# Masking attention scores on VectorE instead of TensorE, with the steps of the loop written out

## The reference

```python
qkv = jnp.einsum('btc,oc->bto', x, w_qkv)            # x: 16 sequences of 512 tokens, 128 channels
q, k, v = ...                                        # 16 heads of 8 channels
attn = jnp.einsum('bhqd,bhkd->bhqk', q, k) / math.sqrt(DK)
mask = jnp.abs(idx[None, :] - idx[:, None]) > 128
attn = jnp.where(mask[None, None], -1000000000.0, attn)
p = jax.nn.softmax(attn, axis=-1)
out = jnp.einsum('bhqk,bhkd->bhqd', p, v)
```

## Time and profile before

| what | value |
|---|---|
| median of the runs | 1780.42 us (1779.67, 1780.42, 1784.23) |
| the profiled execution's own time | 1781.27 us |
| its span, first to last instruction | 1779.6 us |
| TensorE busy | 1539.2 us, 86% of the span |
| VectorE busy | 1477.4 us, 83% |
| GpSimd busy | 1328.7 us, 75% |
| ScalarE busy | 1266.0 us, 71% |
| one full step of the attention, t = 3 to 14 | 43.06 us (516.68 us from 170.50 to 687.18, 12 steps) |

### The profile page before, as it was taken

How to read it: one execution, slowest core, us unless ns; L and a number is a source line. 1 busy time by engine, 2 the same in 40 slices (tenths; PEclk the granted TensorE clock), 3 DMA queues, 4 the chain that set the end, 5 groups by cost and what they waited for, 6 DMA issues and landing times.

```text
span 1779.6 us, 35628 instructions
## 1 busy us (share of the span) xinstructions
PE 1539.2 (86%) x11712; PEld 1100.6 (62%) x11712; DVE 1477.4 (83%) x3720; ACT 1266.0 (71%) x1741; POOL 1328.7 (75%) x1579
## 2 busy tenths in 40 slices
PE   3899999999999999868888888888888888888887
PEld 2455655656555665426666676766666676766666
DVE  3767888888878887339999999999999999999998
ACT  1156666666666666638888888888888888888885
POOL 1045555555555555639999999999999999999993
PEclk9789999999999999969999999999999999999999
DMA  5334444444444443010000000000000000000000
GB/s 143 78 82 93 101 101 99 100 97 97 97 97 105 97 97 84 27 54 1 19 18 2 19 19 1 19 19 19 1 19 19 9 10 19 19 1 19 13 7 7
DMA packets 73436, 85.62 MB, mean 48 GB/s; under 512 B 9856, under 2 KB 63616, under 8 KB 68608
## 3 DMA queue, kind: packets, MB, share of 16 engines
q1 hardware_dynamic: 73312, 84.08, 20.1%
HBM read 58.10 MB, written 25.95 MB: 47 GB/s over the span
## 4 chain that ended last, share of the span: by engine, by line
POOL 31%; issue 7%; DVE 7%; ACT 6%; PE 5%; DVEq 0%; ACTq 0%; SPq 0%
POOL SUM L746 31%; DVE W L939 5%; PE WT L1007 3%; ACT E L847 3%; ACT L781 1%; PE MB L949 1%; ACT GE L780 1%; DVE M8Y L883 0%; PE MB L952 0%; DVE SMALL L900 0%; ACT SIM L774 0%; PE MB L974 0%; DVE CT L922 0%; PE E L962 0%; ACT OUT L794 0%
## 5 line engine op out<-in xcount | busy, mean ns | idle before, releaser
L746 POOL TENSOR_TENSOR SUM<-SIM 128x1024 f32<-128x1024 f32 x512 | 958.0, 1913 | 9.5 <-DVE W L939 5.5
L939 DVE SCALAR_TENSOR_TENSOR W<-SUM,SMALL,E 128x1024 f32<-128x1024 f32 x512 | 641.6, 1279 | 45.8 <-ACT E L847 43.8
L847 ACT ACTIVATE E<-SUM,NB 128x1024 f32<-128x1024 f32 x512 | 566.8, 1118 | 100.1 <-DVE W L939 89.8
L1007 PEld LDWEIGHTS WT<-idf,W 128*128 128x128 f32 x4096 | 488.7, 149 | 237.9 <-DVE W L939 124.3
L1007 PE MATMUL WT<-idf,W 128*128 128x128 f32 x4096 | 559.9, 288 | 70.8 <-DVE CT L922 38.0
L264 POOL TENSOR_SCALAR_AFFINE_SELECT PT<-PT 128x128 f32<-128x128 f32 (+1 forms) x1024 | 334.6, 351 | 319.4 <-ACT PT L354 283.0
L409 DVE TENSOR_REDUCE mx<-SX 128x2 f32<-128x512 f32 x256 | 175.3, 685 | 105.1 <-PE SX L492 104.3
L411 DVE TENSOR_REDUCE mx<-SY 128x2 f32<-128x768 f32 x256 | 242.4, 947 | 7.3 <-PE SY L492 6.9
L354 ACT ACTIVATE PT<-TX 128x512 f32<-128x512 f32 x256 | 152.9, 597 | 98.5 <-PE TX L519 97.1
L356 ACT ACTIVATE PT<-TY 128x768 f32<-128x768 f32 x256 | 207.2, 809 | 1.5
L488 PE MATMUL SY<-K,Q 72*128 72x384 bf16 x512 | 164.0, 343 | 16.4 <-DVE mx L411 15.7
(11 more groups left out here) (111 smaller groups left out, 1663.3 us busy)
## 6 DMA issues: line engine op xcount, KB each, us to landing
K<-k_parts SPq DMA_DIRECT2D x96, 192.0 KB
Q<-q_parts SPq DMA_DIRECT2D x288, 64.0 KB
q_parts<-qp SPq DMA_DIRECT2D x16, 384.0 KB, 2.4
k_parts<-kp SPq DMA_DIRECT2D x16, 384.0 KB, 2.4
xin<-in_x SPq DMA_DIRECT2D x16, 256.0 KB, 3.1
xres<-in_x SPq DMA_DIRECT2D x16, 256.0 KB, 9.4
x<-X SPq DMA_DIRECT2D x16, 256.0 KB, 2.2
x2T<-X2T SPq DMA_DIRECT2D x16, 256.0 KB, 2.1
```

Of the source, the lines that this page charges most:

```text
L746: return eng.tensor_tensor(SUM[(q * FH + h) % RING][:, :].rearrange("p (i j) -> p i j", i=NK), sx, sy, ALU.add)
L847: nc.scalar.activation(E[h % 2][:, :], SUM[(k * FH + h) % RING][:, :], ACT.Exp, bias=NB[q][:, h:h + 1]).then_inc(S["exp_ready"], 1)
L939: nc.vector.scalar_tensor_tensor(out=W[h % WRING][:, :], in0=SUM[(k * FH + h) % RING][:, :], scalar=TOP[q][:, h, TOPK - 1:TOPK], in1=E[h % ...
L1007: o = pe.matmul(WT[:, e, :], W[h % WRING][:, e * P:(e + 1) * P], ident[:, :], is_transpose=True, start=(h == 0 and e % 4 == 0), stop=(h == ...
```

## The change

VectorE now adds the mask itself. One instruction adds a band from SBUF (`bandf`, 0 and -1e30 in 32 bits) to the scores, writes the sum back to where the scores were in PSUM, and keeps the maximum. It works on one product at a time, so a head has four of them instead of two reductions. TensorE's mask products are gone. The inner scores and the inner maxima are signalled one product at a time instead of two at once, so all counts of `inner_maxima` are doubled. All 18 steps are written out. The constants are three bands in one array of 192 KB in place of `idb` (32 KB) and `bandb` (64 KB), and VectorE waits for the constants before its first instruction.

```diff
     def steps(eng, do):
-        for t in (-1, 0, 1):
-            do(t, t)
-        with eng.Fori(0, 6) as i:
-            do(i * 2 + 2, 2)
-            do(i * 2 + 3, 3)
-        for t in (14, 15, 16, 17):
+        for t in range(-1, SEQS + 2):
             do(t, t)
...
-        for dst, src in ((wq[:, :], w_qkvT), (wp[:, :], w_projT), (idb[:, :], identb), (bandb[:, :], band)):
+        for dst, src in ((wq[:, :], w_qkvT), (wp[:, :], w_projT), (bandf[:, :], bands)):
...
+        def masked_max(scores, k0, k1, out):
+            return nc.vector.tensor_tensor_reduce(out=scores, in0=scores, in1=bandf[:, k0 * P:k1 * P], scale=1.0,
+                                                  scalar=-3e38, op0=ALU.add, op1=ALU.max, accum_out=out)
+        dve.wait_ge(S["consts_loaded"], 64)
...
-                    nc.vector.tensor_reduce(mx[:, h, 0:4:3], SX[:, :, :], AX.X, ALU.max).then_inc(S["outer_maxima"], 1)
-                    dve.wait_ge(S["inner_scores"], n)
-                    nc.vector.tensor_reduce(mx[:, h, 1:3], SY[:, :, 0:384], AX.X, ALU.max).then_inc(S["inner_maxima"], 1)
+                    masked_max(SX[:, 0, :], 1, 3, mx[:, h, 0:1])
+                    masked_max(SX[:, 1, :], 0, 2, mx[:, h, 3:4]).then_inc(S["outer_maxima"], 1)
+                    dve.wait_ge(S["inner_scores"], 2 * n - 1)
+                    masked_max(SY[:, 0, 0:3 * P], 0, 3, mx[:, h, 1:2]).then_inc(S["inner_maxima"], 1)
+                    dve.wait_ge(S["inner_scores"], 2 * n)
+                    masked_max(SY[:, 1, 0:3 * P], 0, 3, mx[:, h, 2:3]).then_inc(S["inner_maxima"], 1)
...
             tile(SX[:, 0, :], 0, 0, 2)
-            tile(SX[:, 1, :], 3, 2, 4, False)
-
-            outside(SX[:, :, :].rearrange("p j n -> p (j n)")[:, P:3 * P], bandb[:, :]).then_inc(S["outer_scores"], 1)
-            if c > 0 or h > 0:
-                pe.wait_ge(S["inner_maxima"], n - 1)
-            for n, i in enumerate((1, 2)):
-                tile(SY[:, n, 0:3 * P], i, i - 1, i + 2)
-                outside(SY[:, n, 0:P], LO)
-                o = outside(SY[:, n, 2 * P:3 * P], HI)
-            o.then_inc(S["inner_scores"], 1)
+            tile(SX[:, 1, :], 3, 2, 4).then_inc(S["outer_scores"], 1)
+            for e, i in enumerate((1, 2)):
+                if c > 0 or h > 0:
+                    pe.wait_ge(S["inner_maxima"], 2 * n - 3 + e)
+                tile(SY[:, e, 0:3 * P], i, i - 1, i + 2).then_inc(S["inner_scores"], 1)
```

More of the change, by code:

```diff
@@ L50, with attention @@
 VSUB = TILES * H // 2 * SLOT_V
-def attention(nc, ctx, x, w_qkvT, w_projT, identb, band, w_q, keysT, idf, bnst, KM, extra, x1_out, x2T_out, first):
+def attention(nc, ctx, x, w_qkvT, w_projT, bands, w_q, keysT, idf, bnst, KM, extra, x1_out, x2T_out, first):
     def sb(name, shape, dt=F32):
@@ L74, in attention @@
     KT = sb("KT", [P, 2 * FH * NK])
-    idb = sb("idb", [P, P], BF16)
-    bandb = sb("bandb", [P, 2 * P], BF16)
+    bandf = sb("bandf", [P, 3 * P])
     xin = [sb(f"xin{b}", [P, TILES, P]) for b in range(2)]
@@ L473, in _ @@
     def _(pe):
-        pe.wait_ge(S["consts_loaded"], 80)
+        pe.wait_ge(S["consts_loaded"], 64)
         pe.wait_ge(S["v_pads_set"], 5)
-        HI, LO = bandb[:, 0:P], bandb[:, P:2 * P]
         def scores(t, c, h):
@@ L485, in scores, with tile @@
                 pe.wait_ge(S["heads_8_15_loaded"], 192 * (t + 1))
[L487 to L492, removed]
+            def tile(out, i, k0, k1):
+                return pe.matmul(out, Q[b][0:KQ, h, i * P:(i + 1) * P], K[b][0:KQ, h, k0 * P:k1 * P],
+                                 start=True, stop=True, skip_group_check=True)
             if c > 0 or h > 0:
@@ L557, in step @@
                     bank_free(pe, "mt1", t, c)
-                    pe.wait_ge(S["inner_maxima"], t * H)
+                    pe.wait_ge(S["inner_maxima"], t * H * 2)
                     pe.transpose(MB[0:HT, 0, :], mx[:, 8:16, :].rearrange("p h i -> p (h i)"), idf[:, :]).then_inc(S["maxima_turned"], 1)
@@ L561, in step @@
                     bank_free(pe, "mt0", t, c)
-                    pe.wait_ge(S["inner_maxima"], t * H + 8)
+                    pe.wait_ge(S["inner_maxima"], t * H * 2 + 16)
                     pe.transpose(MB[0:HT, 0, :], mx[:, 0:8, :].rearrange("p h i -> p (h i)"), idf[:, :]).then_inc(S["maxima_turned"], 1)
@@ L1013, in _, with program @@
         outputs(GROUPS * GT - 1, GROUPS - 1, 1, GT - 1)
-def program(nc, x, w_qkvT, w_projT, ident, identb, band, w_q, keysT, key_inT, key_out, gb, out):
+def program(nc, x, w_qkvT, w_projT, ident, bands, w_q, keysT, key_inT, key_out, gb, out):
     x1 = nc.dram_tensor("x1", (SEQS * T, P), F32, kind="Internal").ap()
@@ L1031, in program @@
         with ExitStack() as ctx:
-            attention(nc, ctx, x, w_qkvT, w_projT, identb, band, w_q, keysT, idf, bnst, KM, extra, x1, x2T, first)
+            attention(nc, ctx, x, w_qkvT, w_projT, bands, w_q, keysT, idf, bnst, KM, extra, x1, x2T, first)
         with ExitStack() as ctx:
@@ L1038 @@
            L0_ffn_key_in, L0_ffn_key_out):
-    import ml_dtypes
     import numpy as np
@@ L1054 @@
         "ident": np.eye(P, dtype=np.float32),
-        "identb": np.eye(P, dtype=np.float32).astype(ml_dtypes.bfloat16),
-        "band": np.concatenate([np.where(keep.T, 0, -1e30), np.where(keep, 0, -1e30)], axis=1).astype(ml_dtypes.bfloat16),
+        "bands": np.concatenate([np.where(keep, 0, -1e30), np.zeros((P, P)), np.where(keep.T, 0, -1e30)], axis=1).astype(np.float32),
         "w_q": np.asarray(L0_ffn_w_q),
```

## The result

The changed kernel takes 1853.41 us in the median of four runs (1849.76 to 1855.63), the kernel before 1780.05 in four (1778.82 to 1784.23): a ratio of 1.0406, 95% interval 1.0387 to 1.0424. It is 4% slower. The forecast of 1839 is 14 us too low, the range of 1785 to 1910 held. (PSUM, named throughout, is the memory into which TensorE writes its products; `SX`, `SY`, `TX` and `TY` lie there.)

The account below looks back on a forecast made before the run. Neither engine alone bounds a step: VectorE and TensorE exchange SX and SY, VectorE's chain mostly last. Terms 27 - 1.5 - 4 + 2 = +23.5, plus +35 for the clock, give +58.5 on 1781.27: median 1839 us, range 1785 to 1910.

Parts of the forecast that it names:

- The masked head: On VectorE, two additions at 0.33, two at 0.46 and four read-outs at 0.10 us: 1.98 a head, 0.52 more.
- rival C: On VectorE, the read-out of the maximum hides behind the next addition: 1.58 us a head, 1759 us; chance 0.11.
- The slots at full clock: In attention steps 3 to 15, slot changes without clock falls sum to +2.1 us a step, +27 in all.
- TensorE's gain: On TensorE, the dropped mask products free 0.33 us a head, 5.3 us a step.
- The clock: TensorE's clock falls once in each of steps 2 to 15, at 2.5 us a fall: +35 us.
- The other terms: Outside the full steps: later start, steps 0 to 2, steps behind 14; writing out the loop counted as nothing.
- the start: VectorE's first instruction waits for the constants, so the first scores come later: +2 us.
- Steps 0 and 1: In the first two steps TensorE is last in many slots, so its gain counts: -4 us, between 0 and -10.
- step 2: The step whose clock fell already before the change: from 46.67 us to 45.2, -1.5 us.
- What was looked for: Signs: VectorE busy above 90%, trs not waited for; clocks of 0.9, SX waits over 3 us in slots 3 and 11.
- B: Rival: TensorE's clock holds in the attention steps; 1804 us, down to 1785; chance 0.22.
- D: Rival: VectorE's added instructions do not overlap, 2.62 us a head; 1912 us; chance 0.21.

Follow-up runs that it names:

- e11: The changed kernel with spare TensorE columns only in slots where they should be free (none ahead of SX in slots 3, 5, 6, 7, 11, 14); 1793.84 us.
- e6: The kernel before without mask products, maxima over unmasked scores, with 768 spare columns ahead of SX in twelve slots (all but 5, 6, 7, 14); 1778.88 us.
- e8: e7 with 512 spare TensorE columns ahead of SX in slots 15, 0, 1, 8 and 9; 1764.95 us.
- e3: The kernel before with its 18 steps written out, nothing else; 1781.04 us, ratio 0.9980.
- e4: The kernel before without its mask products, maxima taken over unmasked scores; 1803.98 us, ratio 1.0101.
- e9: e8 with heads 11 and 15 masked on VectorE as well; 1763.00 us.
- e7: The kernel before with steps written out and masks on VectorE only in heads 2, 5, 6, 7, 10 and 14, no spare work; 1771.20 us.
- e2: The changed kernel with 768 spare TensorE columns ahead of SX in slots 15, 0, 1, 2, 8, 9 and 10 only; 1816.47 us.
- e5: The changed kernel with 768 spare TensorE columns ahead of SX in twelve slots (all but 5, 6, 7 and 14); 1831.56 us.
- e10: e5 with 1280 spare columns instead of 768 in slots 3 and 4; 1810.72 us.
- e1: The changed kernel with as many spare TensorE columns in each head as the masks had, ahead of the SX and SY products; 1803.94 us.

## Why the prediction was right, step by step

It named the cause, the falls of the clock, and the side; that its number came so close is in part luck. For the twelve full steps it had 12 x (2.1 + 2.5) = +55.2 us, and they take 54.0 more, but two of its terms there were wrong by about as much in opposite directions. The changed kernel's own sum: 2.5 + 3.3 + 2.6 + 54.0 + 11.9 = 74.3 us, where +58.5 was forecast; what the forecast lacks lies in steps 0 to 2 and behind step 14. The table groups the slots as the prediction did. Each number is the time in us from VectorE's first maximum of one head to that of the next, the median over steps 3 to 14; for e11, e6 and e8 it is over slots at full clock alone.

| slots | before | predicted change | changed | e11, at full clock | e6, short heads | e8, mixed |
|---|---|---|---|---|---|---|
| 0, 3, 8, 13 | 11.33 | +2.1 | 12.48 | 12.39 | 11.36 | 11.28 |
| 1 and 2 | 5.63 | 0 | 8.15 | 5.47 | 5.63 | 5.40 |
| 9 and 10 | 5.64 | 0 | 7.92 | 5.49 | 5.62 | 5.41 |
| 4 to 7 | 10.70 | -0.4 | 9.85 | 9.86 | 9.67 | 9.67 |
| 14 | 3.21 | -0.2 | 2.84 | 2.84 | 2.93 | 3.27 |
| 11, 12, 15 | 6.55 | +0.6 | 6.52 | 6.82 | 6.41 | 6.38 |
| step | 43.06 | +2.1 | 47.76 | 42.87 | 41.62 | 41.41 |

- **The masked head**: 1.98 us predicted, 1.74 measured. The additions were right: 0.33 from start to start for the first, and 0.51 to 0.52 for the wide ones with a read-out beside them, 0.46 without its 0.05. The read-out was not. It starts with the next addition and costs 0.05 us, not 0.10. That is 0.28 more than before instead of 0.52, and it lies just at the 1.75 us that rival C named as the point at which loss and gain meet.
- **The slots at full clock**: +2.1 us a step predicted; e11 gives -0.2. Slots 0, 3, 8 and 13 cost 1.15 us instead of 2.1, about four times 0.28. Slots 4 to 7 give back 0.85, twice the forecast, 14 gives 0.37, and each pair with a values product 0.15 to 0.16, where the later release was thought to eat it. Slots 11, 12 and 15 cost nothing; the 0.3 in e11's column are its spare columns ahead of `SX` of head 12. This is the step of the sum that failed in size: its 13 x 2.1 = +27 should have been about zero.
- **TensorE's gain**, 5.3 us a step: the products are gone, but in e6, with part of its spare columns paid for, only 1.4 us a step shows as time where the clock holds (43.06 against 41.62).
- **The clock**: one fall a step at 2.5 us predicted. The price was right: slot 2 is 5.09 us in the changed kernel and 2.41 in e11, slot 10 is 5.32 and 2.89, so a fall costs 2.68 and 2.43. There are two a step, not one: the prediction had called slots 8 and 9 "alike", held two falls to be the upper bound, and took one. Two are 5.1 us a step; the measured rise is 4.7 (47.76 - 43.06), and the slots give back the rest. This term was sized too small, by about as much as the one above was too large: +35 was predicted for steps 2 to 15, and two falls in each of the twelve full ones alone are 12 x 5.1 = 61.
- **The other terms**: the start was +2 and is +2.5. In runs without that wait the first maxima come at 39.5 to 40.8 (e3, e4, e6 to e9), 39.40 before, so up to 1.4 of the 2.5 need not be the wait's. Steps 0 and 1 were -4 and are +3.3; step 2 was -1.5 and is +2.6; steps 15 to 17, for which one more step of +2.1 and a fall were counted, are +10.9. Step 0 is as long as it was (40.2 us); in step 1 two of the three values products run at about half rate (the row below has one; none did before), so what TensorE gained does not show, and steps 2 and 15 have falls like the full ones. Behind step 14 seven of nine values products are slowed, 12.4 us together over their 2.36, where before it was one, 2.1 us; that is close to the +10.9, though no run takes it apart. Writing out the steps is nothing, by e3.

One values product of step 1 on TensorE, start and duration; 2.36 us is the time at full clock:

```profile
100.45 4.27 PE L539 MATMUL PV<-PT,V 128*32 128x256 f32 x32
```

- **What was looked for**: waits for `SX` above 3 us in slots 3 and 11, a clock below 0.9 in the attention, and no wait for `trs` are all there. VectorE's busy share above 90% is not: it is 83%, since VectorE waits out the falls (in e11, with five falls, it is 473.51 of 523.11 us, 91%).
- **The rivals**: B, that the clock holds, is refuted by the trace and by e4. The Trainium skill, "TensorE: Matmul & The Clock Gate", section "Loop structure matters more than you think", lets matmuls stay warm across VectorE's emptying of PSUM. The runs bear that out only in part: with the masks of six heads off TensorE the clock held in eight of twelve steps (e7), with those of all sixteen in none (the changed kernel). There no wait was long: no pause of TensorE ahead of the falls of steps 4 to 14 is above 0.78 us. C has its mechanism confirmed in part: the read-out hides but for 0.05 us, and the gain stays small. D, nothing overlaps, is refuted by the starts: the trace has each read-out and the next addition start at the same time. The Trainium skill, "VectorE: DVE Perf Modes", section "The DRAIN you can't avoid", would by its first rule put each read-out behind its addition and the next addition behind that. The same section of the Trainium skill adds that an operation that is not held starts earlier, which the prediction left out. (The advice to keep operations few, which the prediction puts there, stands in that page of the Trainium skill under "Rules for kernel authors".) The trace agrees with that addition: 322.37 is the start of both.

What stays open: which of the light slots loses the clock differs from kernel to kernel (1 and 8 in the changed kernel, 4 in e2 and e5, 9 in e11, none in e8), and no run here tells what decides it. That more work ahead of slot 4 makes the falls there fewer is seen in e10 against e5 (three and nine of twelve steps, 1810.72 and 1831.56 us); that e1, with the same 768 columns spread over `SX` and `SY`, lost the clock three times and e5 nine is not explained.

## What to carry to other kernels

Before work is taken off TensorE, look at what it does in the slots where it already waits: there the work was free, and it may be what keeps the clock up for the long products behind it. Move such work slot by slot, off the engine only where that engine ends the slot (here six heads of sixteen were 0.7% faster, 0.8% with spare columns, where all sixteen were 4% slower). Price a chain of dependent small instructions by distances from start to start, never by durations from a table of lines.

## What the hardware showed that was not expected

Taking the 768 mask columns off TensorE, of 3328 a head (the scores, made twice, and the masks), and nothing else, made the program 1.0% slower (e4). Adding columns whose results nobody reads made the changed kernel about 50 us faster (e1). A read-out of the accumulator, 140 ns by its record, starts together with the next addition and costs it 0.05 us. An addition with one operand in PSUM, the other in SBUF and the sum back to PSUM takes 0.33 us for 256 columns from start to start, and for 384 columns 0.51 to 0.52 with a read-out beside it, 0.46 without the read-out's 0.05.
